# Scan block of a Mamba layer: exponentials of the decays written to SBUF, decay tiles multiplied in pairs

## The chip, the cores and the metric

One Trainium2 chip, one core of it. The time is the device time of one execution of the whole kernel in microseconds; the kernel before was run three times without the profiler, and one more execution was profiled.

## The reference

The kernel computes a decoder of four layers, each with three parts that are added to a residual x of 8 batches x 128 tokens x 128 features. The change touches only the first part, a Mamba block. Cut to what matters, with delta = softplus(...), u = silu(conv(...)) of 256 channels, and 64 states for each channel:

```python
A = -jnp.exp(A_log)
def step(h, inputs):
    d_t, B_t, C_t, u_t = inputs
    dA = jnp.exp(d_t[:, :, None] * A)
    h = h * dA + (d_t * u_t)[:, :, None] * B_t[:, None, :]
    y_t = jnp.einsum('bdn,bn->bd', h, C_t)
    return (h, y_t)
```

For each of 8 batches, 256 channels and 64 states there is a recurrence over 128 tokens: h is multiplied by the decay exp(delta * A), then delta * u * B is added; y sums h * C over the states.

## The kernel before, in words

`mamba_stage` (from L836) runs a norm, `mamba_inputs` (projections, convolution, softplus), `scan_block` (L1059), and `mamba_output` (gate, output projection, and early work of the next part). Engines run their own instruction streams and meet at semaphores.

`scan_block` works on 128 tiles: 8 batches (b) x 2 channel halves (c) x 8 tiles. A tile has 16 channels: its 128 partitions hold 2 channels (j) x 64 states, and its free axis 2 (s) x 4 (i) channels x 128 tokens, 1024 elements of 4 bytes. `place` (L1085) maps tile k to (b, c, side, q); side picks the lower or the upper 64 channels of a half. A unit is the 8 tiles of one (b, c). What each engine does for tile k:

- SP (L1088): waits until the scan of k-7 is done, then issues two DMAs that bring du = delta * u, each row spread over 64 partitions, from `du_rows` in HBM to one of the seven `ring` areas (XN, XNT, O, masked_cos, masked_sin, and two halves of pos_bias, all in SBUF and free at this time).
- POOL (L1106): multiplies the ring area by B in place (L1111) and counts `fed`.
- PE (L1114): `multiply(k)` makes A * delta, 8 products with a contraction over 32 rows each, into one of three PSUM areas `decay` (two banks each). It waits for `scanned` of k-3, since the scan reads the area. The 32 rows come from two of the four row strips, g = 2 side + s.
- ACT (L1171): takes the exponential in place in PSUM (L1200) and counts `decayed`.
- DVE (L1209): one `tensor_tensor_scan` (L1219) over the 1024 elements, state = decay * state + fed, from the PSUM area and the ring area to the buffer `h` of the unit (small_pack or h1, alternating). Token 0 of each channel has decay 0, set once by a memset of a column (L1211), which makes one instruction of the eight recurrences.

Once a unit is scanned, PE sums h * C over the states: `gather(n, part)` (L1131), 128 products of 32 columns, in four parts that stand behind the multiplications of four tiles. `Cz` holds C placed in zeros by ACT (`place_c`, L1172). ACT copies the sum (`copy_sum`), PE turns it back and adds D * u (`turn_back`, L1147), and ACT copies y over du (`copy_y`). The order on PE is the loop at L1162, on ACT the one at L1196; POOL, DVE and SP go tile by tile.

The prediction also speaks of three places outside the scan: the convolution (L974, DVE, with POOL preparing A_pairs and D_order in L1012 and L1014), du = delta * u (L1002, DVE), and the gate product of `mamba_output` (L1035, DVE) beside which POOL makes masked_cos and masked_sin (L794).

## Time and profile before

| | us |
|---|---|
| three runs, median (lowest to highest) | 1407.34 (1396.89 to 1410.18) |
| profiled execution, its own time | 1392.82 |
| span in the profile, first to last instruction | 1390.8 |
| PE busy, over the whole span | 1114.5 (80%) |
| DVE busy | 850.9 (61%) |
| POOL busy | 570.0 (41%) |
| ACT busy | 529.5 (38%) |

The mean granted clock of TensorE is 0.848 of 2.4 GHz. The page gives busy time and the costliest groups over the whole span; since the parts of the kernel have different limits, the scan block is read from windows, from the groups by line and from the timeline of its own stretch. In the timeline each line is one instruction or a merged run of them: its start, its length, the engine, the line of the code, what is written from what, and in brackets how long the engine had been idle and what it waited for. In the trace a fp32 product shows as two MATMUL records, so the 8 products of a tile are "x16".

### The profile page before, as it was taken

The numbers are of one execution on the slowest core, as the hardware profiler recorded it, in microseconds if no ns is written. First come the engines' busy times: TensorE is split into PE (matmuls) and PEld (weight loads), VectorE is DVE, ScalarE is ACT, GpSimd is POOL, SyncE is SP. The second block draws the span as 40 slices with busy tenths as digits, with TensorE's granted clock in tenths as the row PEclk, the third lists the DMA queues.
The fourth block names the chain that finished last, engine by engine and source line by source line (L and its number), as shares of the span: only waits on it lengthen the run. The fifth ranks groups of instructions, "written<-read, shape, count | busy, mean of one in ns | idle before, by whom it ended". The sixth has DMA issues, their size and how long they took to land. (4 is left out here: it accounts for less than half of the span.)

```text
span 1390.8 us, 29830 instructions
## 1 busy us (share of the span) xinstructions
PE 1114.5 (80%) x12054; PEld 800.1 (58%) x12065; DVE 850.9 (61%) x1500; ACT 529.5 (38%) x1322; POOL 570.0 (41%) x382
## 2 busy tenths in 40 slices
PE   5568898898887898999547598689476899866895
PEld 2158787887875454545336255545366454543695
DVE  6577888888884476366713476567512676755233
ACT  2433434434431363255114164156133565612121
POOL 4169988989864702210157310020434201000432
PEclk9656988888878599999869799699688998987998
DMA  2099687778855200000075100000365000000793
GB/s 105 0 207 216 196 214 206 203 208 211 204 168 198 65 1 1 0 1 2 1 201 182 33 2 1 1 1 1 116 199 185 1 2 1 1 1 23 259 302 99
DMA packets 74232, 139.75 MB, mean 100 GB/s; under 512 B 8129, under 2 KB 28369, under 8 KB 73745
## 3 DMA queue, kind: packets, MB, share of 16 engines
q1 hardware_dynamic: 70128, 129.67, 32.8%
q0 software_dynamic: 3968, 8.18, 1.6%
q8 instruction: 96, 1.57, 0.5%
q14 instruction: 40, 0.32, 0.1%
HBM read 128.06 MB, written 14.82 MB: 103 GB/s over the span
## 5 line engine op out<-in xcount | busy, mean ns | idle before, releaser
L658 ACT ACTIVATE shifted_a<-scores,nmax_a 128x128 f32<-128x128 f32 x768 | 208.5, 387 | 85.7 <-DVE nmax_a L624 85.7
L1125 PE MATMUL decay<-delta,A_pairs 32*128 32x127 f32 x2048 | 178.6, 335 | 49.2 <-DVE small_pack L1219 18.9
L1200 ACT ACTIVATE decay<-decay 128x1016 f32<-128x1016 f32 x128 | 128.7, 1010 | 197.8 <-PE decay L1125 197.8
L1125 PEld LDWEIGHTS decay<-delta,A_pairs 32*128 32x128 f32 x2048 | 155.5, 235 | 69.6 <-DVE small_pack L1219 23.6
L624 DVE TENSOR_REDUCE nmax_a<-scores 128x4 f32<-128x512 f32 x192 | 123.6, 686 | 108.3 <-PE scores L563 105.9
L361 POOL TENSOR_TENSOR rstd<-ve,neghalf 128x4 f32<-128x4 f32 x30 | 31.5, 1051 | 281.7 <-DVE ve L347 281.7
L630 DVE COPY PTs_a<-PT 128x512 f32<-128x512 f32 x192 | 123.6, 681 | 4.6 <-PE PT L571 4.6
L571 PE MATMUL PT<-mamba_pack,shifted_a 128*128 128x128 f32 x768 | 114.1, 293 | 4.3 <-DVE PTs_a L630 2.7
L1460 POOL DMA_INDIRECT results<-xs_s x76 | 73.0, 960 | 104.2 <-DVE xs_s L1632 96.6
L571 PEld LDWEIGHTS PT<-mamba_pack,shifted_a 128*128 128x128 f32 x768 | 88.5, 149 | 36.8 <-issue 20.1
L247 PE MATMUL norm_ps<-identb 128*128 128x512 bf16 x180 | 59.6, 446 | 52.2 <-DVE ve L347 51.5
L1111 POOL TENSOR_TENSOR pos_bias<-pos_bias,B 128x1024 f32<-128x1024 f32 x36 | 85.2, 2383 | 6.8 <-DMA pos_bias<-du_rows 6.7
L563 PE MATMUL scores<-KH_a,QT_a 32*128 32x512 f32 x256 | 76.4, 674 | 1.0 <-POOL KH_a L547 1.0
L580 PEld LDWEIGHTS PO<-PTs_a,V 128*32 128x32 f32 x1536 | 37.3, 111 | 64.3 <-issue 35.2
L547 POOL TENSOR_TENSOR KH_a<-KT_a,small_pack 128x512 f32<-128x512 f32 x24 | 24.9, 1041 | 119.6 <-PE scores L563 100.4
L1142 PE MATMUL Y<-small_pack,Cz 128*32 128x64 f32 x2048 | 63.2, 288 | 1.9 <-issue 1.9
L1142 PE MATMUL Y<-h,Cz 128*32 128x64 f32 x2048 | 62.8, 288 | 1.6 <-issue 1.0
L1111 POOL TENSOR_TENSOR XN<-XN,B 128x1024 f32<-128x1024 f32 x19 | 45.1, 2374 | 45.6 <-DMA XN<-du_rows 45.5
L580 PE MATMUL PO<-PTs_a,V 128*32 128x128 f32 x1536 | 62.4, 284 | 0.0
L247 PEld LDWEIGHTS norm_ps<-identb 128*128 128x128 bf16 x180 | 19.4, 113 | 74.2 <-DVE ve L347 54.7
L329 ACT ACTIVATE XNT<-norm_ps 128x512 f32<-128x512 f32 x12 | 7.2, 597 | 140.6 <-PE norm_ps L369 140.6
L1142 PEld LDWEIGHTS Y<-small_pack,Cz 128*32 128x32 f32 x2048 | 54.8, 134 | 7.2 <-issue 5.3
(395 smaller groups left out, 2238.3 us busy)
## 6 DMA issues: line engine op xcount, KB each, us to landing
pos_bias<-du_rows SPq DMA_DIRECT2D x72, 256.0 KB, 4.9
small_pack<-L3f_w SPq DMA_DIRECT2D x15, 768.0 KB, 5.0
XN<-du_rows SPq DMA_DIRECT2D x38, 256.0 KB, 5.1
XNT<-du_rows SPq DMA_DIRECT2D x38, 256.0 KB, 4.8
O<-du_rows SPq DMA_DIRECT2D x36, 256.0 KB, 4.9
masked_cos<-du_rows SPq DMA_DIRECT2D x36, 256.0 KB, 4.9
masked_sin<-du_rows SPq DMA_DIRECT2D x36, 256.0 KB, 4.8
small_pack<-L2f_w SPq DMA_DIRECT2D x15, 514.0 KB, 5.0
```

Of the source, the lines that this page charges most:

```text
L247: nc.tensor.matmul(out, m.identb[:], bcast_mid(m.identb[:], HG), start=True, stop=True)
L563: nc.tensor.matmul(scores[u % 4][:], QT[rows, b * S:(b + 1) * S], KH[b % 2][rows, :, :], start=False, stop=True).then_inc(m.scored, 1)
L571: t = nc.tensor.transpose(PT[u % 2][:, j, :], shifted[u % 4][:, j, :], ident)
L580: t = nc.tensor.matmul(PO[32 * j:32 * j + 32, g, :], m.V[:, b, g * HG + j, :], PTs[u % 4][:, j, :], start=True, stop=True)
L624: nc.vector.tensor_reduce(nmax[:, u % 4, :], scores[u % 4][:], AX.X, ALU.min).then_inc(m.maxed, 1)
L630: nc.vector.tensor_copy(PTs[u % 4][:], PT[u % 2][:]).then_inc(m.pt_copied, 1)
L658: t = nc.scalar.activation(shifted[u % 4][:, j, :], scores[u % 4][:, j, :], ACT.Exp, scale=-1.0, bias=nmax[:, u % 4, j:j + 1])
L1111: nc.gpsimd.tensor_tensor(x, x, bcast_mid(B2[:, b * S:(b + 1) * S], PER), ALU.mult).then_inc(fed, 1)
L1125: t = nc.tensor.matmul(decay[k % DEEP][:, s, i, 1:S], A_pairs[strip, c, 4 * q + i, :, :].rearrange("p j n -> p (j n)"), delta[strip, c, b ...
L1142: t = nc.tensor.matmul(Y[32 * i:32 * i + 32, n % 2, half, :], Cz[:, token, :], at_token[n % 2][:, :, token], start=(turn == 0), stop=(turn ...
L1200: nc.scalar.activation(x, x, ACT.Exp).then_inc(decayed, 1)
L1460: nc.gpsimd.indirect_dma_start(results, bass.IndirectOffsetOnAxis(ap=number, axis=0), xs[:, j, 0:D], None).then_inc(returned.sem, returned ...
```

## The change

The seven areas are split: the first two (XN and XNT) become `kept`, and the exponential writes from PSUM to `kept[k % 2]`; the ring for the fed values keeps five. The scan reads `kept` and the ring. PSUM areas are given back by ACT (`decayed`) instead of DVE (`scanned`), and ACT waits for the scan of k-2, whose `kept` area it takes. `place` is changed so that tiles 2p and 2p+1 are the two sides of one q, and `multiply(p)` makes both, 16 products that go around the four row strips, into two PSUM areas. The gather of a unit is cut into parts of 9, 9, 9 and 5 turns of four products (8 each before), one behind each pair; the copies on ACT move accordingly.

```diff
@@ -1063,7 +1063,8 @@
 
 
 
-    UNITS, PER, DEEP = B * IC, 8, 3
+    UNITS, PER, DEEP, KEPT = B * IC, 8, 3, 2
+    TURNS = [0, 9, 18, 27, 32]
     TILES = UNITS * PER
     with ExitStack() as ctx:
         sb = lambda name, shape, dt=F32: ctx.enter_context(nc.sbuf_tensor(name, shape, dt))
@@ -1072,8 +1073,9 @@
         flat = lambda a: a.rearrange("p b d -> p (b d)")
         ring = [flat(m.XN[:]), m.XNT[:], flat(m.O[:]), flat(m.masked_cos[:]), flat(m.masked_sin[:]),
                 flat(m.pos_bias[:, 0:H // 2, :]), flat(m.pos_bias[:, H // 2:, :])]
+        ring = [a.rearrange("p (s i t) -> p s i t", s=2, i=4) for a in ring]
+        ring, kept = ring[KEPT:], ring[:KEPT]
         R = len(ring)
-        ring = [a.rearrange("p (s i t) -> p s i t", s=2, i=4) for a in ring]
         Ys = [sb(f"Ys{k}", [128, 2, PAIRS]) for k in range(2)]
         decay = [ctx.enter_context(nc.psum_tensor(f"decay{k}", [128, 2, 4, S], F32)) for k in range(DEEP)]
         Y = ctx.enter_context(nc.psum_tensor("Y", [128, 4, 2, PAIRS], F32))
@@ -1082,7 +1084,7 @@
         multiplied, decayed, fed, scanned, c_placed, summed, sum_copied, sum_turned, y_copied, zeroed = (
             m.sem(f"scan_{n}") for n in ("multiplied", "decayed", "fed", "scanned", "c_placed", "summed",
                                          "sum_copied", "sum_turned", "y_copied", "zeroed"))
-        place = lambda k: (k // (2 * PER), k // PER % 2, k % PER // 4, k % 4)
+        place = lambda k: (k // (2 * PER), k // PER % 2, k % 2, k % PER // 2)
         block = ctx.enter_context(nc.Block())
 
         @block.sync
@@ -1112,21 +1114,20 @@
 
         @block.tensor
         def _(pe):
-            def multiply(k):
-                b, c, side, q = place(k)
-                if k >= DEEP:
-                    pe.wait_ge(scanned, k - DEEP + 1)
-                else:
-                    pe.wait_ge(zeroed, DEEP)
+            def multiply(p):
+                if 2 * p + 2 > DEEP:
+                    pe.wait_ge(decayed, 2 * p + 2 - DEEP)
+                b, c, _, q = place(2 * p)
                 for i in range(4):
-                    for s in range(2):
-                        g = 2 * side + s
+                    for g in range(4):
+                        side, s = g // 2, g % 2
                         strip = slice(32 * g, 32 * g + 32)
                         t = nc.tensor.matmul(
-                            decay[k % DEEP][:, s, i, 1:S],
+                            decay[(2 * p + side) % DEEP][:, s, i, 1:S],
                             A_pairs[strip, c, 4 * q + i, :, :].rearrange("p j n -> p (j n)"),
                             delta[strip, c, b * S + 1:(b + 1) * S], start=True, stop=True)
-                t.then_inc(multiplied, 1)
+                        if i == 3 and s == 1:
+                            t.then_inc(multiplied, 1)
 
             def gather(n, part):
                 b = n // IC
@@ -1135,12 +1136,12 @@
                     pe.wait_ge(c_placed, b + 1)
                     if n >= 2:
                         pe.wait_ge(sum_copied, n - 1)
-                half = part // 2
-                for turn in range(8 * (part % 2), 8 * (part % 2) + 8):
+                for turn in range(TURNS[part], TURNS[part + 1]):
+                    half = turn // 16
                     for i in range(4):
-                        token = 64 * half + 16 * i + turn
+                        token = 64 * half + 16 * i + turn % 16
                         t = nc.tensor.matmul(Y[32 * i:32 * i + 32, n % 2, half, :], Cz[:, token, :],
-                                             at_token[n % 2][:, :, token], start=(turn == 0), stop=(turn == 15))
+                                             at_token[n % 2][:, :, token], start=(turn % 16 == 0), stop=(turn % 16 == 15))
                 if part == 3:
                     t.then_inc(summed, 1)
 
@@ -1159,13 +1160,13 @@
                                              m.w("alternate")[:, rows], start=False, stop=True)
                 t.then_inc(sum_turned, 1)
 
-            for k in range(TILES + 18):
-                if k < TILES:
-                    multiply(k)
-                if k >= 11 and (k - 11) % 8 < 4 and (k - 11) // 8 < UNITS:
-                    gather((k - 11) // 8, (k - 11) % 8)
-                if k >= 17 and (k - 17) % 8 == 0 and (k - 17) // 8 < UNITS:
-                    turn_back((k - 17) // 8)
+            for p in range(TILES // 2 + 6):
+                if p < TILES // 2:
+                    multiply(p)
+                if p >= 9 and p % 4 == 1:
+                    turn_back((p - 9) // 4)
+                if p >= 5 and (p - 5) // 4 < UNITS:
+                    gather((p - 5) // 4, (p - 5) % 4)
 
         @block.scalar
         def _(act):
@@ -1193,30 +1194,35 @@
                 nc.scalar.activation(du[:, c, b * S:(b + 1) * S], YT[:, n % 2, :], ACT.Copy).then_inc(y_copied, 1)
 
             place_c(0)
-            for k in range(TILES + 19):
+            for k in range(TILES + 13):
                 if k < TILES:
                     act.wait_ge(multiplied, k + 1)
-                    x = decay[k % DEEP][:, :, :, 1:S].rearrange("p s i t -> p (s i) t")
-                    nc.scalar.activation(x, x, ACT.Exp).then_inc(decayed, 1)
-                if k % 16 == 8 and 0 < k // 16 < B:
+                    if k >= KEPT:
+                        act.wait_ge(scanned, k - KEPT + 1)
+                    else:
+                        act.wait_ge(zeroed, k + 1)
+                    nc.scalar.activation(kept[k % KEPT][:, :, :, 1:S].rearrange("p s i t -> p (s i) t"),
+                                         decay[k % DEEP][:, :, :, 1:S].rearrange("p s i t -> p (s i) t"),
+                                         ACT.Exp).then_inc(decayed, 1)
+                if k % 16 == 10 and 0 < k // 16 < B:
                     place_c(k // 16)
-                if k >= 15 and (k - 15) % 8 == 0 and (k - 15) // 8 < UNITS:
-                    copy_sum((k - 15) // 8)
-                if k >= 18 and (k - 18) % 8 == 0 and (k - 18) // 8 < UNITS:
-                    copy_y((k - 18) // 8)
+                if k >= 17 and k % 8 == 1 and (k - 17) // 8 < UNITS:
+                    copy_sum((k - 17) // 8)
+                if k >= 20 and k % 8 == 4 and (k - 20) // 8 < UNITS:
+                    copy_y((k - 20) // 8)
 
         @block.vector
         def _(dve):
-            for k in range(DEEP):
-                nc.vector.memset(decay[k][:, :, :, 0:1], 0.0).then_inc(zeroed, 1)
+            for k in range(KEPT):
+                nc.vector.memset(kept[k][:, :, :, 0:1], 0.0).then_inc(zeroed, 1)
             for k in range(TILES):
-                n = k // PER
-                out = h[n % 2][:, k % PER * T:(k % PER + 1) * T]
+                n, (_, _, side, q) = k // PER, place(k)
+                out = h[n % 2][:, (4 * side + q) * T:(4 * side + q + 1) * T]
                 dve.wait_ge(decayed, k + 1)
                 dve.wait_ge(fed, k + 1)
                 if n >= 2 and k % PER == 0:
                     dve.wait_ge(summed, n - 1)
-                nc.vector.tensor_tensor_scan(out, decay[k % DEEP][:].rearrange("p s i t -> p (s i t)"),
+                nc.vector.tensor_tensor_scan(out, kept[k % KEPT][:].rearrange("p s i t -> p (s i t)"),
                                              ring[k % R].rearrange("p s i t -> p (s i t)"), 0.0, ALU.mult,
                                              ALU.add).then_inc(scanned, 1)
 
```

On PE, at the start of the scan block, there stand before (each product shows one row, 128x127; `waits` names the semaphore):

```order
L1125 MATMUL decay<-delta,A_pairs 128x127 [waits scan_scanned]
L1125 MATMUL decay<-delta,A_pairs 128x127 x7
L1142 MATMUL Y<-small_pack,Cz 32x64 [waits scan_c_placed,scan_scanned]
L1142 MATMUL Y<-small_pack,Cz 32x64 x31
L1125 MATMUL decay<-delta,A_pairs 128x127 [waits scan_scanned]
L1125 MATMUL decay<-delta,A_pairs 128x127 x7
L1142 MATMUL Y<-small_pack,Cz 32x64 x32
```

and now:

```order
L1125 MATMUL decay<-delta,A_pairs 128x127 [waits scan_decayed]
L1125 MATMUL decay<-delta,A_pairs 128x127 x15
L1143 MATMUL Y<-small_pack,Cz 32x64 [waits scan_c_placed,scan_scanned]
L1143 MATMUL Y<-small_pack,Cz 32x64 x35
L1125 MATMUL decay<-delta,A_pairs 128x127 [waits scan_decayed]
L1125 MATMUL decay<-delta,A_pairs 128x127 x15
L1143 MATMUL Y<-small_pack,Cz 32x64 x36
```

Two tiles are multiplied in a row, the wait is on ACT's count, and a gather part has 36 products.

On DVE (the scan is listed as SCALAR_TENSOR_TENSOR) the first scans of the block were:

```order
L1211 MEMSET decay 128x8 x3
L1219 SCALAR_TENSOR_TENSOR small_pack<-decay,XN 128x1024 [waits scan_fed,scan_decayed]
L1219 SCALAR_TENSOR_TENSOR small_pack<-decay,XNT 128x1024 [waits scan_fed,scan_decayed]
L1219 SCALAR_TENSOR_TENSOR small_pack<-decay,O 128x1024 [waits scan_fed,scan_decayed]
L1219 SCALAR_TENSOR_TENSOR small_pack<-decay,masked_cos 128x1024 [waits scan_fed,scan_decayed]
```

and are now:

```order
L1217 MEMSET XN 128x8
L1217 MEMSET XNT 128x8
L1225 SCALAR_TENSOR_TENSOR small_pack<-XN,O 128x1024 [waits scan_fed,scan_decayed]
L1225 SCALAR_TENSOR_TENSOR small_pack<-XNT,masked_cos 128x1024 [waits scan_fed,scan_decayed]
L1225 SCALAR_TENSOR_TENSOR small_pack<-XN,masked_sin 128x1024 [waits scan_fed,scan_decayed]
L1225 SCALAR_TENSOR_TENSOR small_pack<-XNT,pos_bias 128x1024 [waits scan_fed,scan_decayed]
```

The number of scans and what they wait for are the same; their first input was PSUM (`decay`) and is SBUF (XN or XNT).

On ACT, in the middle of the block, the exponentials with the copies between them stood as follows:

```order
L1200 ACTIVATE decay<-decay 128x8x127 [waits scan_multiplied] x5
L1185 ACTIVATE Ys<-Y 128x128 [waits scan_summed]
L1200 ACTIVATE decay<-decay 128x8x127 [waits scan_multiplied] x3
L1193 ACTIVATE du<-YT 128x128 [waits scan_sum_turned]
```

and stand there now, with the placing of C (`Cz`) a tile further back:

```order
L1204 ACTIVATE XNT<-decay 128x8x127 [waits scan_scanned,scan_multiplied]
L1186 ACTIVATE Ys<-Y 128x128 [waits scan_summed]
L1204 ACTIVATE XN<-decay 128x8x127 [waits scan_scanned,scan_multiplied]
L1180 ACTIVATE Cz<-C 64x8x16 [waits scan_summed]
L1180 ACTIVATE Cz<-C 64x8x16
L1204 ACTIVATE XNT<-decay 128x8x127 [waits scan_scanned,scan_multiplied]
```

Each exponential had one wait, on PE's count, and has a second, on DVE's; it writes XN or XNT.

## Rows read from the trace of the kernel before

**Rows 1.** Windows of the kernel before: busy us of PE, PEld, DVE, ACT, POOL (xcount), PEclk, DMA share, GB/s
```profile
95.00:100.00 5.00, 4.53 (x36) 3.68 (x34) 4.96 (x3) 2.00 (x2) 5.00 (x3) 0.50 1.07 235
140.00:150.00 10.00, 9.11 (x220) 8.15 (x216) 7.92 (x5) 5.30 (x8) 8.09 (x4) 1.00 0.67 186
81.60:416.40 334.80, 297.79 (x6080) 266.67 (x6080) 285.79 (x128) 136.28 (x170) 300.27 (x128) 0.79 0.80 204
```

**Rows 2.** Timeline, first and last tile of the scan: start, length in us, engine, line
```profile
81.65 2.34 POOL L1111 TENSOR_TENSOR XN<-XN,B 128x1024 f32<-128x1024 f32 x1 [42.34 <-DMA XN<-du_rows]
...
414.12 2.29 DVE L1219 TENSOR_TENSOR_SCAN h<-decay,XNT 128x1024 f32<-128x1024 f32 x1 [0.69 <-ACT decay L1200]
```

**Rows 3.** Groups by line and shape, 0 to 420 us: busy us, mean ns, idle before, releaser
```profile
L1125 PE MATMUL decay<-delta,A_pairs 32*128 32x127 f32 x2048 | 178.6, 335 | 49.2 <-DVE small_pack L1219 18.9 <-DVE decay L1211 15.7 <-DVE h L1219 12.9
...
L1200 ACT ACTIVATE decay<-decay 128x1016 f32<-128x1016 f32 x128 | 128.7, 1010 | 197.8 <-PE decay L1125 197.8
...
L1111 POOL TENSOR_TENSOR XNT<-XNT,B 128x1024 f32<-128x1024 f32 x19 | 45.2, 2379 | 4.1 <-DMA XNT<-du_rows 4.0
...
L1219 DVE TENSOR_TENSOR_SCAN small_pack<-decay,XNT 128x1024 f32<-128x1024 f32 x9 | 20.5, 2275 | 2.7 <-ACT decay L1200 2.7
...
L1002 DVE TENSOR_TENSOR du<-delta,u 128x1024 f32<-128x1024 f32 x2 | 2.5, 1226 | 0.1
...
L932 ACT ACTIVATE u<-conv 128x1024 f32<-128x1024 f32 x2 | 2.1, 1048 | 8.5 <-DVE conv L974 8.5
```

**Rows 4.** Timeline, steady stretches of the scan block, all engines
```profile
93.31 1.23 SPq L1099 DMA_DIRECT2D masked_cos<-du_rows  x2
...
102.58 2.08 PE L1125 MATMUL decay<-delta,A_pairs 32*128 32x127 f32 x16 [0.22 <-DVE small_pack L1219]
...
106.88 1.99 PE L1142 MATMUL Y<-small_pack,Cz 128*32 128x64 f32 x64
...
107.55 2.38 POOL L1111 TENSOR_TENSOR masked_sin<-masked_sin,B 128x1024 f32<-128x1024 f32 x1
...
107.69 2.29 DVE L1219 TENSOR_TENSOR_SCAN h<-decay,masked_cos 128x1024 f32<-128x1024 f32 x1 [0.57 <-POOL masked_cos L1111]
...
411.88 1.16 PE L1125 MATMUL decay<-delta,A_pairs 32*128 32x127 f32 x16
```

**Rows 5.** Timeline, DVE and POOL behind the scan block, instruction by instruction
```profile
429.96 0.69 DVE L1035 TENSOR_TENSOR du<-du,gate 128x512 f32<-128x512 f32 x1 [13.54 <-PEq L1068]
430.56 0.68 DVE L1035 TENSOR_TENSOR du<-du,gate 128x512 f32<-128x512 f32 x1
431.07 2.03 POOL L794 TENSOR_TENSOR masked_cos<-O,small_pack 128x1024 f32<-128x1024 f32 x1 [0.50 <-ACT O L777]
431.17 2.49 DVE L1035 TENSOR_TENSOR du<-du,gate 128x512 f32<-128x512 f32 x1
433.07 2.44 POOL L794 TENSOR_TENSOR masked_sin<-O,small_pack 128x1024 f32<-128x1024 f32 x1
433.58 2.48 DVE L1035 TENSOR_TENSOR du<-du,gate 128x512 f32<-128x512 f32 x1
```

**Rows 6.** Timeline, DVE and POOL in the convolution
```profile
34.52 3.78 POOL L1012 TENSOR_TENSOR A_pairs<-A,mamba_pack 128x2048 f32<-128x2048 f32 x1
34.74 4.10 DVE L974 SCALAR_TENSOR_TENSOR conv<-padded,mamba_pack,conv 128x512 f32<-128x512 f32 x1
42.44 0.73 DVE L974 SCALAR_TENSOR_TENSOR conv<-padded,mamba_pack,conv 128x512 f32<-128x512 f32 x1
```

**Rows 7.** Groups by line, 75 to 430 us, and the page's DMA issues (KB, us to landing)
```profile
L1156 PE MATMUL YT<-u,D_order 128*64 128x64 f32 x128 | 15.0, 250 | 1.7 <-ACT Ys L1185 1.7
...
O<-du_rows SPq DMA_DIRECT2D x36, 256.0 KB, 4.9
```

**Rows 8.** Line L1219: what DVE waited for before its scans, us and times
```profile
  ACT decay L1200: 45.6, 47
  POOL XN L1111: 8.1, 1
```

## The prediction

> **What bounds the kernel now.** I read the page first: five engines, none busy over 80%, and the two costliest lines of the first third are in the scan block. The stage windows come next [rows 1]. The scan stage proper runs from the first POOL multiplication at 81.65 us to the end of the last scan, 414.12 + 2.29 = 416.4 us [rows 2]: 334.8 us for 128 tiles, 2.62 us a tile. In it POOL is busy 300.3 us, DVE 285.8 and PE 297.8. So three engines are near their limits and none is at it.
>
> The groups by line give what one tile costs [rows 3]: POOL multiplies by B in 2.38 us, DVE scans in 2.28 us, ACT takes the exponentials in 1.01 us, and PE makes the products. What DVE waits for is ACT, 45.6 us over 47 waits, against 8.1 us for POOL, all at the first tile [rows 8]; ACT waits 197.8 us for PE [rows 3]. The ring of waits is: the scan of tile k-3 frees a PSUM area, PE multiplies (2.08 us, or 1.16 us at the full clock [rows 4]), ACT exponentiates, DVE scans. When PE also gathers (1.99 us a part, in front of the next multiplication), the ring is late and DVE idles. The timeline shows the other thing that matters: the POOL multiplication and the scan run at the same time, POOL from 107.55 for 2.38 us and DVE from 107.69 for 2.29 us, both at their usual length [rows 4]. The stage lives from this overlap, since POOL and DVE together need 2.38 + 2.28 = 4.65 us a tile and get 2.62.
>
> **What the change removes.** PSUM areas are free after ACT (1.01 us) instead of after the scan (2.28 us), so PE runs ahead and the 45.6 us that DVE waits for ACT should go. Left alone, that makes POOL the bound: 128 x 2.377 = 304.3 us plus one last scan, 306.5 us, 28 us less than now.
>
> **What it adds: a scan with both inputs in SBUF.** So far the scan reads the decays from PSUM and the fed values from SBUF. Now it reads XN or XNT, and O or another ring area: two tensors in SBUF. No scan of this trace does that, so its cost is bounded from other instructions with two SBUF inputs that meet a POOL instruction reading SBUF. There are two places, and both say the same.
>
> At 430 us DVE multiplies du by gate, 512 elements, both in SBUF [rows 5]. The second of the four takes 0.68 us. The third starts at 431.17, just behind a POOL multiplication (431.07 for 2.03, so to 433.10), and takes 2.49 us: it ends at 433.66, 0.56 after POOL. The next POOL multiplication, same shape, starts at 433.07 while DVE is at work, and takes 2.44 us instead of 2.03: it ends at 435.51, 1.85 after DVE. The fourth DVE one starts at 433.58 and takes 2.48 us, to 436.06, 0.55 after POOL. So the two alternate and nothing overlaps but the ends: DVE saves 0.68 - 0.55 = 0.13 us of its own length and POOL 2.03 - 1.85 = 0.18. In the convolution the same [rows 6]: a DVE instruction of 0.73 us takes 4.10 us (34.74 to 38.84) behind a POOL one of 3.78 us (34.52 to 38.30), and ends 0.54 after it.
>
> The Trainium skill, page SBUF — State Buffer, section Who interferes with whom, states this as a rule: a VectorE instruction with two SBUF inputs fetches the second through the read interface that it shares with GpSimd, and against a GpSimd instruction that reads SBUF the later one is blocked fully until the first ends. The trace agrees (2.49 us for 0.68). Taken to the letter, without the saving at the ends, the rule gives the upper bound below.
>
> Applied to a tile: scan 2.276 - 0.13 = 2.14, POOL 2.377 - 0.18 = 2.19, together 4.33 us. They alternate, since the finished engine's next instruction queues behind the waiting one. The order of POOL and DVE changes in nothing but names and operands. Stage: first POOL multiplication alone 2.34, then 127 x 2.19 = 278.1, 127 scans x 2.14 = 271.8, last scan 2.28: 554.5 us. Against 334.8: **+219.7 us**. Ends of this term: above, no saving, 127 x 4.65 + 4.6 = 595.6, +261; below, both savings 0.2, as DVE's in the convolution (0.73 - 0.54), and POOL at its shortest (2.34 [rows 2]), 127 x (2.08 + 2.14) + 4.6 = 540, +205. I take the middle one because its rows have the same kind of POOL instruction and a full cycle.
>
> **The other edits, at 4.33 us a tile.** All cost nothing, and the slack is what hides them.
> - ACT writes SBUF instead of PSUM. The u row, 1024 elements SBUF to SBUF, is 1.05 us [rows 3]; 1.01 now. Bounds 0 to 0.05 us on an engine busy 1.0 of 4.33.
> - ACT now waits for the scan of k-2. Behind it stand the next exponential, the copies of Y and the placing of C; PE (for its PSUM area) and DVE wait for them. Exponential k can start when scan k-2 ends and is ready 1.05 later; scan k wants it 4.33 after that end. Slack 3.3 us, more than a copy's wait for one gather part (2.2 us).
> - PE works on pairs: 16 products over four row strips, then 36 gather products instead of 32. If four strips overlap no better than two, a pair costs 2 x 2.08 = 4.16 at 1.2 GHz, a part 1.99 x 36/32 = 2.24, turning back 1.9 us once in four pairs (twice the 15.0 us of one of its two lines, for 16 units [rows 7]): at most 8.3 us in the pair that has it and 6.4 in the others, of 8.66. If they do, less. It now waits for exponential 2p-2, which ends some 1.1 us after scan 2p-4; the product is needed by exponential 2p, when scan 2p-2 ends, 8.66 later. Cover goes only if the tile is under some 3 us. The clock here is 0.50 to 1.00 of 2.4 GHz [rows 1], and the sum above is with 1.2 GHz, so a colder PE is in it.
> - The ring has five areas for seven. A turn is scan end, 1.22 us issue [rows 4], 4.9 us to landing [rows 7], POOL and DVE 4.33, some 10.5 us; five tiles last 21.7. The DMA engines, at 1.07 of their time at 2.3 us a tile [rows 1], fall to about half.
> - Tile order within a channel pair, areas and the 9, 9, 9, 5 turns of the gather keep all counts. The tail behind the last scan has the same 128 gather products (some 8 us), so it stays at 13.5 us, to 429.96 [rows 5]. The load of small_pack goes out a few tiles ahead of the end as before.
>
> Sum: 1392.8 (profiled execution) + 219.7 = 1612.5 us. The three plain runs lie 4 to 17 us over the profiled one (median +14.5, 1407.3). Part of that may be waits in the stage that now have slack, so I add half: **1620 us**.
>
> **Rivals.**
> 1. *No blocking: the scan is exempt* and the change does what it removes. For it: the scan fetches slowly, 2.2 ns an element where a two-input multiplication needs 1.2 (1226 ns for 1024 [rows 3]), and no row shows a scan blocked. Against it: both places with two SBUF inputs show full exclusion. Time: stage 306.5 us if refills are all hidden; POOL waits 4.0 us for DMAs at XNT's 19 turns now [rows 3], so some 20 or more over the seven areas, and the ring is shorter, so 306 to 326; 315 gives 1373 in the profile's terms, 1387 as a median. This is the faster side; it decides if POOL keeps 2.38 us beside a scan. Chance 0.07.
> 2. *Shared by turns.* The scan leaves free the slots that it does not fetch in, so it costs POOL only 1.23 - 0.14 = 1.09 us: 2.19 + 1.09 = 3.28 a tile, stage 422, +87, 1480 us (1490 as a median). For it: the same slow fetch. Against it: in the rows one side stands still for all of the other's length. Chance 0.06.
> 3. *The bound moves to PE instead*, by its cold clock and the pair order: 8.3 us in the heaviest pair is under 8.66, so even then under 5 us in all. It is inside the range. That four strips do not run together is priced in there too; it changes nothing.
>
> On the first rival, the Trainium skill, page DVE: opcode table, instruction layouts, handler registers and perf-mode slots, section Datapath and trigger behaviour, says that the built-in tensor_tensor_scan carries a value back to an earlier stage and so runs at half throughput. The trace agrees (2276 ns for 1024 elements). The page doesn't say whether the read interface is held meanwhile; were it free half the time, the second rival's 1480 would follow.
>
> **How the numbers follow.** Forecast 0.86, first rival 0.07, second 0.06, else 0.01. Range of the forecast: 1598 (lower term) to 1654 (upper), with 0 to 17 us for the plain runs above; I give 1594 to 1660, which leaves out the rivals' 0.13. A measurement here tells about 1% from no change. Faster by over 1%: 0.06 (first rival but for its slow end), same 0.01, slower 0.93.
>
> **What would show it.** In the changed kernel's profile: scans or POOL multiplications of some 4.3 us at steady places, each ending 2.1 to 2.2 us behind the other's end, with both engines reported busy nearly throughout; the stage 555 us long; DMA share about 0.45; DVE's idle time for ACT gone; PE waiting for ACT. Scans of 2.28 beside POOL's 2.38 would prove me wrong, with the first rival; 3.3 us a tile, the second. If a tile takes over 4.7 us, some wait that I gave slack decides.

## The result, and the profile after

| | before | after |
|---|---|---|
| runs, median (lowest to highest), us | 1406.58 (1396.89 to 1410.18), 4 runs | 1624.16 (1619.73 to 1628.76), 4 runs |
| profiled execution, its own time | 1392.82 | 1619.73 |
| span | 1390.8 | 1618.0 |
| granted clock, mean of the span | 0.848 | 0.786 |

The kernel is slower by 15.6%: the ratio is 1.1558, with an interval of 1.1514 to 1.1601. The forecast was 1620 us, in a range of 1594 to 1660.

The timeline of the kernel after, some 220 us into the stage, answers to [rows 4]: start, length, engine, line, and in brackets the idle time before and its releaser.

```profile
299.23 4.33 POOL L1113 TENSOR_TENSOR masked_sin<-masked_sin,B 128x1024 f32<-128x1024 f32 x1
301.34 4.37 DVE L1225 TENSOR_TENSOR_SCAN small_pack<-XNT,masked_cos 128x1024 f32<-128x1024 f32 x1
...
301.51 1.02 ACT L1204 ACTIVATE XN<-decay 128x1016 f32<-128x1016 f32 x1 [3.29 <-DVE small_pack L1225]
...
302.58 2.09 PE L1125 MATMUL decay<-delta,A_pairs 32*128 32x127 f32 x32 [4.63 <-ACT XN L1204]
303.52 8.66 POOL L1113 TENSOR_TENSOR pos_bias<-pos_bias,B 128x1024 f32<-128x1024 f32 x2
...
305.63 4.40 DVE L1225 TENSOR_TENSOR_SCAN small_pack<-XN,masked_sin 128x1024 f32<-128x1024 f32 x1
```

POOL ends at 303.56, the scan at 305.71 (2.15 later), the next scan begins at 305.63. Both engines have nearly doubled lengths and no gap between instructions: a busy engine here is one that stands in line. That is the trap of this profile, because the shares of busy time say "DVE and POOL are fully used", while each works half of the time. The start of the stage shows which of the two is standing.

Timeline of the kernel after, first tiles and last scan:

```profile
79.41 2.34 POOL L1113 TENSOR_TENSOR O<-O,B 128x1024 f32<-128x1024 f32 x1 [42.48 <-DMA O<-du_rows]
81.84 2.29 DVE L1225 TENSOR_TENSOR_SCAN small_pack<-XN,O 128x1024 f32<-128x1024 f32 x1 [8.21 <-POOL O L1113]
81.90 4.38 POOL L1113 TENSOR_TENSOR masked_cos<-masked_cos,B 128x1024 f32<-128x1024 f32 x1 [0.16 <-DMA masked_cos<-du_rows]
...
86.24 2.35 POOL L1113 TENSOR_TENSOR masked_sin<-masked_sin,B 128x1024 f32<-128x1024 f32 x1
86.38 4.35 DVE L1225 TENSOR_TENSOR_SCAN small_pack<-XNT,masked_cos 128x1024 f32<-128x1024 f32 x1 [2.25 <-POOL masked_cos L1113]
...
627.95 2.26 DVE L1225 TENSOR_TENSOR_SCAN h<-XNT,masked_sin 128x1024 f32<-128x1024 f32 x1
```

The first scan begins 0.06 us before the second multiplication. It keeps its 2.29 us, and POOL takes 4.38 and ends 2.15 behind it. At 86.24 the order is the other way round: POOL, 0.14 us earlier, keeps 2.35, and the scan takes 4.35 and ends 2.14 behind POOL. So whoever starts first is undisturbed and the other gets all of the wait. From then on each instruction starts while the other engine is at work, and each pays: from the scan at 94.94 to the one at 619.38, 122 tiles later, it is 524.44 / 122 = 4.30 us a tile. The last scan, with no multiplication beside it, is back at 2.26.

The stage lasts from 79.41 to 627.95 + 2.26 = 630.2, which is 550.8 us against 334.8 [rows 2].

The scan line's waits in the kernel after (us, times), and who waited for it, answer to [rows 8]:

```profile
  POOL O L1113: 8.2, 1
  POOL masked_cos L1113: 2.2, 1
...
  ACT XN L1204: 207.2, 63
  ACT XNT L1204: 200.6, 63
```

The 45.6 us for ACT [rows 8] are gone, as intended, and ACT now waits for DVE. The same stretch in the groups by line (75 to 660 us: busy us, mean ns, idle before), and the window:

```profile
L1113 POOL TENSOR_TENSOR pos_bias<-pos_bias,B 128x1024 f32<-128x1024 f32 x50 | 215.9, 4338 | 0.0
L1125 PE MATMUL decay<-delta,A_pairs 32*128 32x127 f32 x2028 | 121.2, 406 | 224.9 <-ACT XN L1204 224.9
...
L1204 ACT ACTIVATE XN<-decay 128x1016 f32<-128x1016 f32 x64 | 65.1, 1017 | 207.2 <-DVE small_pack L1225 106.9 <-DVE h L1225 100.3
```

```profile
75.00:660.00 585.00, 283.48 (x6448) 247.97 (x6445) 561.09 (x165) 146.87 (x180) 558.76 (x142) 0.64 0.45 130
```

The exponential into SBUF takes 1.017 us (1.010 in place [rows 3]). PE waits 224.9 us and its granted clock over the stretch is 0.64 (0.63 over the stage alone, against 0.79 [rows 1]); in the trace nobody waits for its products. The DMA share is 0.45 (0.46 over the stage alone, against 0.80 [rows 1]), and the page has 4.3 us from issue to landing for O (4.9 [rows 7]).

The account of the spans, 1618.0 - 1390.8 = 227.2 us: the stage +216.0; its start 2.2 earlier; the tail between the last scan and the first gate product 9.4 us for 13.5, so -4.2; and the rest of the kernel behind that product 978.4 us for 960.8, +17.6. The last is probably not the change's: the code there is the same, and so is the granted clock, 0.87 in both traces. The kernels of the experiments below, the same in this part too, spend 950.2 to 982.1 us in it, by chip 970.6 to 982.1 (four traces), 955.7 to 966.0 (four), 950.2 to 963.7 (three) and 981.1 (one). Within one chip that is at most 13.4 us, less than the 17.6; but the whole kernel before varied by 17.4 us over its five executions (1392.82 to 1410.18), and the profiled one was the shortest of them. That chance made the 17.6 is argued from this, not shown. The medians, which smooth it, are 217.6 us apart.

### The profile page after: what moved, and what is told of

Read it like the earlier page. It is cut to its first block and busy times, and to the rows that moved or that the text cites. A ratio compares the mean times of both kernels' runs of the same rounds, so it can differ in the third digit from the quotient of the medians.

```text
span 1618.0 us, 29957 instructions
## 1 busy us (share of the span) xinstructions
PE 1076.1 (67%) x12054; PEld 761.1 (47%) x12065; DVE 1110.9 (69%) x1499; ACT 531.5 (33%) x1322; POOL 815.4 (50%) x382
## 5 line engine op out<-in xcount | busy, mean ns | idle before, releaser
L1125 PE MATMUL decay<-delta,A_pairs 32*128 32x127 f32 x2048 | 122.4, 406 | 240.4 <-ACT XN L1204 224.9
L1125 PEld LDWEIGHTS decay<-delta,A_pairs 32*128 32x128 f32 x2048 | 105.2, 297 | 256.9 <-ACT XN L1204 239.4
L1113 POOL TENSOR_TENSOR pos_bias<-pos_bias,B 128x1024 f32<-128x1024 f32 x50 | 215.9, 4338 | 0.0
L1204 ACT ACTIVATE XN<-decay 128x1016 f32<-128x1016 f32 x64 | 65.1, 1017 | 207.2 <-DVE small_pack L1225 106.9
L1113 POOL TENSOR_TENSOR O<-O,B 128x1024 f32<-128x1024 f32 x26 | 110.8, 4261 | 42.5 <-DMA O<-du_rows 42.5
L1204 ACT ACTIVATE XNT<-decay 128x1016 f32<-128x1016 f32 x64 | 65.2, 1019 | 200.6 <-DVE small_pack L1225 106.4
L1113 POOL TENSOR_TENSOR masked_cos<-masked_cos,B 128x1024 f32<-128x1024 f32 x26 | 112.9, 4340 | 0.2 <-DMA masked_cos<-du_rows 0.2
L1113 POOL TENSOR_TENSOR masked_sin<-masked_sin,B 128x1024 f32<-128x1024 f32 x26 | 110.8, 4261 | 0.0
```

The costliest lines, as they stand in the source:

```text
L1113: nc.gpsimd.tensor_tensor(x, x, bcast_mid(B2[:, b * S:(b + 1) * S], PER), ALU.mult).then_inc(fed, 1)
L1125: t = nc.tensor.matmul(decay[(2 * p + side) % DEEP][:, s, i, 1:S], A_pairs[strip, c, 4 * q + i, :, :].rearrange("p j n -> p (j n)"), delta ...
L1204: nc.scalar.activation(kept[k % KEPT][:, :, :, 1:S].rearrange("p s i t -> p (s i) t"), decay[k % DEEP][:, :, :, 1:S].rearrange("p s i t -> ...
```

## The experiments

Each was run beside the kernel before on the same chip, whose median differs by chip: 1405.5 us for SBUF alone, pairs alone, the product on DVE and POOL's writes; 1409.6 for the POOL instruction beside a scan from PSUM; 1391.4 to 1391.6 for all others. A ratio is given as it was estimated, with its interval; it can differ by up to 0.4% from the quotient of the two medians. The kernel before alone spreads by 18.6 to 24.1 us on one chip, so where there is one run only, the reading rests on the lengths of the instructions and not on the total. The theory: a scan with two SBUF inputs and a POOL instruction that reads SBUF exclude each other, one whole instruction after the other. Its rivals: the pair order on PE or the shorter ring costs the time; a scan from SBUF is slower by itself; any POOL access to SBUF does it; the two share by turns.

### SBUF areas alone, tile order of before

```diff
-                nc.vector.tensor_tensor_scan(out, decay[k % DEEP][:].rearrange("p s i t -> p (s i t)"),
+                nc.vector.tensor_tensor_scan(out, kept[k % KEPT][:].rearrange("p s i t -> p (s i t)"),
```

With it go the areas `kept`, the exponential's target and the waits of the change; products, gather and copies stay as before.

> Of the change only the two SBUF areas for the exponentials and the waits that go with them; tiles, products, gather and copies in the order of before. Exclusion theory (a scan with both inputs in SBUF and a POOL multiplication don't run at the same time): 4.30 us a tile, scans and multiplications of about 4.35 us, 1612 to 1630 us. Rival, the pair order and PE's new waits cost the time: scans of 2.28 us, about 1400 us.

Measured: 1617.5 us (2 runs), ratio 1.150 (1.143 to 1.157), beside 1.156 for the whole change. POOL and DVE alternate as there (start, length):

```profile
301.44 4.35 POOL L1112 TENSOR_TENSOR masked_sin<-masked_sin,B 128x1024 f32<-128x1024 f32 x1
...
303.57 4.37 DVE L1223 TENSOR_TENSOR_SCAN small_pack<-XNT,masked_cos 128x1024 f32<-128x1024 f32 x1
...
305.74 4.34 POOL L1112 TENSOR_TENSOR pos_bias<-pos_bias,B 128x1024 f32<-128x1024 f32 x1
```

The loss belongs to the areas in SBUF with the ring of five and the waits that go with them; the pair order has no part in it. Two kernels below, with the B product on DVE and with POOL only writing, keep all three and have scans of 2.27 to 2.29 us, so neither the place of the areas nor ring and waits alone make the loss.

### Pairs alone, exponentials in place in PSUM

```diff
-                if k >= DEEP:
-                    pe.wait_ge(scanned, k - DEEP + 1)
+                if 2 * p + 2 > DEEP:
+                    pe.wait_ge(scanned, 2 * p + 2 - DEEP)
```

Seven ring areas, the pair order, the gather parts and copies of the change.

> Of the change only the pairs from four row strips and the gather in four parts behind pairs; exponentials in place in PSUM, ring of seven, PE waits for the scans of 2p-2. Exclusion theory: scans 2.28 us and multiplications 2.38 us side by side; two of three PSUM areas must be free at once, so after scan 2p-2 come 2.09 us of products and 1.01 us of exponential against 2.28 us of the other scan: 2.5 to 2.75 us a tile, 1380 to 1425 us. Rival, the pair order costs the time: over 1550 us.

Measured: 1400.0 us (10 runs), ratio 0.997 (0.993 to 1.001): no difference. Timeline, one pair and the scan beside POOL:

```profile
199.43 2.38 POOL L1112 TENSOR_TENSOR XN<-XN,B 128x1024 f32<-128x1024 f32 x1
199.58 2.26 DVE L1221 TENSOR_TENSOR_SCAN h<-decay,masked_cos 128x1024 f32<-128x1024 f32 x1
...
204.30 1.17 PE L1126 MATMUL decay<-delta,A_pairs 32*128 32x127 f32 x32
```

POOL and the scan start 0.15 us apart and both keep their length. A whole pair, 16 products (x32), takes 1.17 us, as long as one tile of before (x16, 1.16 [rows 4]). The stage takes 326 us from first to last scan (84.5 to 410.65), 332 before. What DVE waits for now:

```profile
  ACT decay L1202: 30.8, 36
  POOL XN L1112: 8.5, 1
  PE Y L1144: 7.6, 14
```

PE lost 66 us of busy time in the window 75 to 430 (312.7 to 246.6), and DVE's wait for ACT only went from 45.6 to 30.8. PE now waits 90.6 us for scans in front of its products, where it waited 31.8 before: there are three areas for tiles made two at a time, a pair needs an area that the scan gives back late, and what PE saves in the products it spends waiting. A kernel with more areas was not run.

### The B product on DVE, POOL idle

```diff
-        @block.gpsimd
-        def _(pool):
-            for k in range(TILES):
...
+            feed(0)
             for k in range(TILES):
+                if k + 1 < TILES:
+                    feed(k + 1)
```

The changed kernel, its POOL instruction given to DVE in front of the scan.

> The changed kernel with the multiplication by B moved from POOL to DVE, one tile ahead of the scan; POOL has nothing to do in the block. Exclusion theory: the scan is 2.28 us again though both its inputs are in SBUF, the multiplication 1.23 us: 3.3 to 3.5 us a tile, about 1500 us, faster than the changed kernel although one engine does the work of two. Rival, a scan from SBUF is slow by itself (4.37 us): 5.5 us a tile, about 1770 us.

Measured: 1492.6 us (one run). Groups by line, one of the scan's forms:

```profile
L1226 DVE TENSOR_TENSOR_SCAN small_pack<-XNT,pos_bias 128x1024 f32<-128x1024 f32 x13 | 29.7, 2288 | 0.0
```

A scan of two SBUF inputs takes 2.29 us when POOL is idle, as one from PSUM does. It isn't slow by itself. The kernel also shows the price of the exclusion in another way: one engine doing both jobs in turn (3.31 us a tile) is 125 us faster than two engines that exclude each other (1617.5 us with the SBUF areas alone, on the same chip).

### POOL only writes

```diff
-                nc.gpsimd.tensor_tensor(x, x, bcast_mid(B2[:, b * S:(b + 1) * S], PER), ALU.mult).then_inc(fed, 1)
+                nc.gpsimd.memset(x, 0.01).then_inc(fed, 1)
```

This kernel leaves out the product with B: the ring is overwritten by a constant.

> The changed kernel with POOL's multiplication by B replaced by a memset of the same tile, so the product du * B is left out: a POOL instruction that writes SBUF and reads nothing. If only POOL's reads exclude the scan: scans of 2.28 us, 2.3 to 2.4 us a tile, 1355 to 1380 us. If any POOL instruction on SBUF does: 2.14 + 0.9 = 3.0 us a tile, about 1455 us. Rival, slow scan from SBUF: 4.3 us a tile, 1620 us.

Measured: 1374.5 us (one run). Timeline:

```profile
202.51 0.95 POOL L1113 MEMSET pos_bias<- 128x1024 f32 x1 [1.28 <-DMA pos_bias<-du_rows]
203.71 2.27 DVE L1225 TENSOR_TENSOR_SCAN small_pack<-XNT,pos_bias 128x1024 f32<-128x1024 f32 x1
...
204.68 0.96 POOL L1113 MEMSET pos_bias<- 128x1024 f32 x1 [1.21 <-DMA pos_bias<-du_rows]
```

The memset at 204.68 lies wholly inside the scan of 203.71 to 205.98, and neither is longer. POOL's writes alone don't collide; with its reads gone the collision is gone. This is what the Trainium skill, page SBUF — State Buffer, section Who interferes with whom, says of a GpSimd instruction that only writes. The run also gives a bound for what the change could be worth without exclusion: DVE's waits between scans fall to 15.5 us behind the first one, and the kernel takes 1374.5 us for 1405.5, but POOL's instruction is shorter here (0.95 us for 2.38). The ring of five areas and the new waits are in this kernel and in the one with POOL idle, so they don't cause the loss.

### POOL reads one operand

```diff
-                nc.gpsimd.memset(x, 0.01).then_inc(fed, 1)
+                nc.gpsimd.tensor_scalar(x, x, 0.01, None, ALU.mult).then_inc(fed, 1)
```

Here too the product with B is left out: a constant takes its place.

> The changed kernel with POOL's multiplication by B replaced by a multiplication with a constant: it reads and writes the same tile but no second tensor, so the product with B is left out. Exclusion theory, in which any POOL instruction that reads SBUF excludes the scan for its length: scans wait, the tile takes 2.14 us plus that instruction's own length (about 1 us for 1024 elements, by the casts of 2048 in 1.9 us), 3.0 to 3.4 us a tile, 1450 to 1510 us. Rival, two tensors on both sides are needed for a collision: scans of 2.28 us, below 1400 us.

Measured: 1430.6 us (one run), below the range that I gave. Timeline, the first tile and a steady place:

```profile
78.00 2.77 POOL L1113 TENSOR_SCALAR O<-O 128x1024 f32<-128x1024 f32 x1 [41.07 <-DMA O<-du_rows]
80.74 2.77 POOL L1113 TENSOR_SCALAR masked_cos<-masked_cos 128x1024 f32<-128x1024 f32 x1
80.87 3.05 DVE L1225 TENSOR_TENSOR_SCAN small_pack<-XN,O 128x1024 f32<-128x1024 f32 x1 [8.80 <-POOL O L1113]
...
199.57 3.00 POOL L1113 TENSOR_SCALAR masked_cos<-masked_cos 128x1024 f32<-128x1024 f32 x1
...
199.93 3.05 DVE L1225 TENSOR_TENSOR_SCAN h<-XN,O 128x1024 f32<-128x1024 f32 x1
...
202.54 3.01 POOL L1113 TENSOR_SCALAR masked_sin<-masked_sin 128x1024 f32<-128x1024 f32 x1
```

At first sight this is the pattern of the changed kernel with smaller numbers, and one could read the 2.98 us of a tile (the mean over the stage; here 199.57 to 202.54) as 2.14 for the scan and 0.84 for a short POOL instruction. The first row forbids it: with no scan beside it, the instruction takes 2.77 us. An exclusion would then need about 2.77 + 2.28 less some 0.3 at the ends, 4.75 us a tile. The scan that starts at 80.87, just behind a POOL instruction, ends 0.41 us behind it (83.92 against 83.51), where one that had stood still would end 2.14 behind. The two run side by side and disturb each other: 0.77 us for the scan, 0.24 for POOL.

The last run settled which of the readings holds.

### The same POOL instruction beside a scan from PSUM

```diff
-                nc.gpsimd.tensor_tensor(x, x, bcast_mid(B2[:, b * S:(b + 1) * S], PER), ALU.mult).then_inc(fed, 1)
+                nc.gpsimd.tensor_scalar(x, x, 0.01, None, ALU.mult).then_inc(fed, 1)
```

The edit is made to the kernel with pairs alone.

> The kernel with pairs alone (decays stay in PSUM, so the scan has one input in SBUF), with POOL's multiplication by B replaced by a multiplication by a constant, one operand read; the product with B is left out. In the earlier kernel with that POOL instruction and the decays in SBUF, the first POOL instruction, with no scan beside it, took 2.77 us, the later ones 3.01 and the scans 3.05, in a period of 2.98 us: much less than the 2.77 + 2.28 - 0.3 = 4.75 of a full exclusion. Theory A: one read operand does collide with the scan's second SBUF input, but only for part of its length (+0.24 us for POOL, +0.77 for the scan). Then here, without the second SBUF input, POOL keeps 2.77 us throughout and the scans 2.28, the tile takes 2.77 us by POOL, the stage 128 x 2.77 + 2.3 = 357 us, and the kernel some 1415 to 1430 us. Theory B: the longer times there have nothing to do with the two reads (the first instruction was short for another reason): POOL takes 3.0 us here too, the stage 386 us, the kernel 1445 to 1460 us. Theory C: such an instruction is about 0.85 us long and the other 2.14 us there were waiting: then POOL's instructions are near 0.85 us here and the stage falls to some 300 us, the kernel to 1370 to 1385.

Measured: 1431.2 us (one run), 1 us over the range of theory A; the instructions are those of theory A, the stage 352.7 us (82.31 to 435.05) for its 357. Timeline, start of the stage and a steady place:

```profile
85.05 2.77 POOL L1112 TENSOR_SCALAR XNT<-XNT 128x1024 f32<-128x1024 f32 x1
85.18 2.29 DVE L1221 TENSOR_TENSOR_SCAN small_pack<-decay,XN 128x1024 f32<-128x1024 f32 x1 [9.02 <-POOL XN L1112]
...
205.43 2.79 POOL L1112 TENSOR_SCALAR masked_cos<-masked_cos 128x1024 f32<-128x1024 f32 x1
205.59 2.29 DVE L1221 TENSOR_TENSOR_SCAN h<-decay,O 128x1024 f32<-128x1024 f32 x1 [0.45 <-POOL O L1112]
```

Without the second SBUF input POOL keeps 2.77 to 2.80 us and the scan 2.29, which waits for POOL (0.45). So theory C, the short instruction, and B fell. One read operand collides with the scan's second SBUF input, but for a part of the time only. The Trainium skill, page SBUF — State Buffer, section Summary: rules for kernel authors, has the second one to issue blocked fully until the first finishes; for the two-operand multiplication the rows agree (4.30 us a tile), for this instruction they don't (2.98, where full blocking would give about 4.75), and the measurement decides. Whether the number of operands or the kind of instruction makes the difference isn't told apart: both changed at once.

### Every second tile through SBUF

```diff
+                    to = kept[k // 2 % KEPT] if k % 2 == 0 else decay[k % DEEP]
...
+                of = kept[k // 2 % KEPT] if k % 2 == 0 else decay[k % DEEP]
```

The lines shown choose the area for the exponential and for the scan; the waits of PE, ACT and DVE are fitted to it.

> The pairs, with the exponentials of even tiles in SBUF and of odd tiles in place in PSUM. Exclusion theory: only the even scans and POOL's multiplications keep each other out, so a pair takes two multiplications of POOL (4.75 us) and one scan of 2.14 us, 6.7 to 6.9 us a pair, half of the way from before to the changed kernel: 1480 to 1515 us. If the stage merely followed PE's order or the ring of five, it would be at one of the ends.

Measured: 1469.8 us (one run), 78 over the kernel before, and 10 below the range that I gave. Timeline of one pair and a bit, DVE and POOL:

```profile
196.66 4.39 DVE L1231 TENSOR_TENSOR_SCAN small_pack<-XNT,pos_bias 128x1024 f32<-128x1024 f32 x1
198.86 4.32 POOL L1113 TENSOR_TENSOR masked_cos<-masked_cos,B 128x1024 f32<-128x1024 f32 x1
200.97 2.26 DVE L1231 TENSOR_TENSOR_SCAN small_pack<-decay,O 128x1024 f32<-128x1024 f32 x1
...
203.14 2.35 POOL L1113 TENSOR_TENSOR masked_sin<-masked_sin,B 128x1024 f32<-128x1024 f32 x1
...
203.28 4.35 DVE L1231 TENSOR_TENSOR_SCAN small_pack<-XN,masked_cos 128x1024 f32<-128x1024 f32 x1
```

In one kernel, beside the same POOL instruction, the scan from PSUM keeps 2.26 us beside POOL and the one from SBUF takes 4.39. The pair takes 6.62 us (196.66 to 203.28), the sum of one excluding round, 2.14 + 2.19, and one free scan, 2.28: 6.61. So the exclusion is priced by instruction, and it can be summed.

### The gather in six parts

What is a better change to the kernel before? Its DVE waits 45.6 us for ACT, when a gather part stands in front of the next products on PE. The first try made the parts smaller and spread them.

```diff
+    TURNS = [0, 6, 12, 17, 22, 27, 32]
...
-                if k >= 11 and (k - 11) % 8 < 4 and (k - 11) // 8 < UNITS:
-                    gather((k - 11) // 8, (k - 11) % 8)
+                if k >= 10 and (k - 10) % 8 < 6 and (k - 10) // 8 < UNITS:
+                    gather((k - 10) // 8, (k - 10) % 8)
```

> The kernel before with the gather of a unit in six parts of 6 or 5 turns behind tiles 10 to 15, instead of four parts of 8 behind tiles 11 to 14. Theory: in before DVE waits for ACT because a gather part of 1.99 us stands in front of the next tile's products; parts of 1.5 us take part of that away, but PE's work stays: 1395 to 1406 us. Rival, the loss is PE's total work at the low clock (about 3.3 us a tile at 1.2 GHz): no gain, 1400 to 1412 us.

Measured: 1455.8 us (4 runs), ratio 1.049 (1.042 to 1.057). The expectation was wrong, theory and rival. Windows, of this kernel and then of the kernel before (busy us of PE, PEld, DVE, ACT, POOL, granted clock, DMA share, GB/s):

```profile
150.00:400.00 250.00, 247.11 (x3927) 220.13 (x3928) 178.47 (x79) 85.46 (x107) 185.33 (x79) 0.50 0.59 166
```

```profile
150.00:400.00 250.00, 225.81 (x4860) 202.59 (x4864) 217.34 (x98) 106.69 (x136) 229.42 (x98) 0.84 0.80 207
```

With the work spread evenly PE is busy 99% of the time at a granted clock of 0.50, which is the 1.2 GHz level, for the whole stretch (and from 90 to 478 us as well). Before, with gaps between its blocks, the mean is 0.84. PE's work for a tile then takes 3.2 us (250 us for 79 scans), and PE is the bound. I had taken the clock for a given. Why the clock stays at the low level here isn't settled by these runs.

### Idle products to hold the clock

Would filling products raise the clock? If they did, they would pay. Two kernels, from the one with pairs alone (gather in 8, 8, 8, 8 turns), put idle bf16 products behind every second pair, four and eight of them. They write to a part of Y that nothing reads.

```diff
+                if p < TILES // 2 and p % 2 == 1:
+                    for _ in range(4):
+                        nc.tensor.matmul(Y[:, 2:4, :, :].rearrange("p a h x -> p a (h x)"), m.identb[:],
+                                         bcast_mid(m.identb[:], 2), start=True, stop=True)
```

> The pairs with exponentials in place in PSUM, and four idle products (128x128 by 256 columns, bf16, into an unused part of the Y area) behind every second pair. Theory: with the scan reading PSUM the stage lives from PE's clock, since a pair takes 2.09 us at 1.2 GHz and 1.17 us at 2.4 GHz between two scans; if the idle products hold the clock up, POOL's 2.38 us a tile is the bound: stage of 308 to 318 us, 1380 to 1392 us. Rival, the clock does not follow them or they only add PE work: 1398 to 1410 us.

> As with four idle products, but eight. If the clock follows activity: at least as high a clock as with four, 1378 to 1392 us, unless the idle products (0.9 us for eight at 2.4 GHz) delay the next pair. Rival: 1400 to 1415 us.

Measured: with four 1396.4 us (10 runs), ratio 1.0005 (0.996 to 1.005); with eight 1418.0 (4 runs), ratio 1.019 (1.012 to 1.025). The windows of the kernel with pairs alone, with four, and with eight:

```profile
150.00:400.00 250.00, 185.78 (x4920) 163.11 (x4916) 218.88 (x99) 104.79 (x136) 230.79 (x100) 0.86 0.77 206
```

```profile
150.00:400.00 250.00, 191.66 (x4897) 160.21 (x4898) 214.65 (x97) 103.19 (x133) 226.02 (x98) 0.84 0.76 204
```

```profile
150.00:400.00 250.00, 200.82 (x4617) 166.98 (x4619) 200.56 (x90) 95.66 (x123) 211.11 (x91) 0.82 0.71 190
```

PE's busy time goes up (185.8, 191.7, 200.8 us) and the granted clock doesn't (0.86, 0.84, 0.82). Two kernels without idle products, below, have 0.82 and 0.87 in this window, so the small steps mean nothing; what is shown is that there is no rise. By its ratio the kernel with four is the rival's, no gain, and the one with eight is 3 us above the rival's range: its products stand in front of the next pair. This theory fell. The pairs-alone kernel shown for comparison has parts of 9, 9, 9 and 5 turns and ran on another chip.

### Larger gather parts

```diff
-    TURNS = [0, 9, 18, 27, 32]
+    TURNS = [0, 10, 20, 30, 32]
```

Pairs alone, with 40 products in three of the parts of a unit and 8 in the last one.

> Pairs with exponentials in place in PSUM, gather parts of 10, 10, 10 and 2 turns for 9, 9, 9 and 5, so that a unit is summed earlier (14 scans waited 7.6 us for it). Theory: a few us off, ratio to before 0.990 to 0.998. Rival, longer parts delay the next pair at 1.2 GHz and take it back: 1.000.

Measured: 1382.7 us (10 runs), ratio 0.9967 (0.993 to 1.0005). Not told apart from the kernel before, nor from the parts of 9, 9, 9 and 5 (0.997). DVE waits 36.0 us for ACT in 40 places, and none for PE (7.6 with the smaller parts).

### Even tiles in halves

The exponentials of a pair come in the order even, odd, and DVE, done with the pair before, waits for the even one: two take 1.91 us, so it comes some 1 us behind PE's end. Here the even tile's exponential and scan are cut at the PSUM bank into two halves, so that the scan of the first half starts when half of the exponential is done. It is the kernel of the experiment before with one more edit.

```diff
-                    x = decay[k % DEEP][:, :, :, 1:S].rearrange("p s i t -> p (s i) t")
-                    nc.scalar.activation(x, x, ACT.Exp).then_inc(decayed, 1)
+                    for banks in (slice(0, 1), slice(1, 2)) if k % 2 == 0 else (slice(0, 2),):
+                        x = decay[k % DEEP][:, banks, :, 1:S].rearrange("p s i t -> p (s i) t")
+                        nc.scalar.activation(x, x, ACT.Exp).then_inc(decayed, 1)
```

> As with parts of 10, 10, 10, 2, and for even tiles the exponential and the scan in two halves of one PSUM bank each, so that the scan starts 0.4 us earlier behind a pair's products (DVE waited for ACT 30.8 us over 36 waits); DVE pays 0.14 us a pair. Theory: 5 to 15 us less than before, ratio 0.985 to 0.997. Rival, POOL at 2.38 us a tile and its DMAs bound it already: 1.000.

Measured: 1374.3 us (6 runs), ratio 0.986 (0.982 to 0.991). It beats both kernels, by 1.4% the one before. Timeline (the halves are merged, x2) and the scan line's waits:

```profile
202.65 1.98 ACT L1203 ACTIVATE decay<-decay 128x508 f32<-128x508 f32 x3 [2.43 <-PE decay L1126]
202.88 2.34 POOL L1112 TENSOR_TENSOR O<-O,B 128x1024 f32<-128x1024 f32 x1
203.49 2.31 DVE L1229 TENSOR_TENSOR_SCAN small_pack<-decay,pos_bias 128x512 f32<-128x512 f32 x2
```

```profile
  ACT decay L1203: 22.1, 35
  POOL XN L1112: 8.7, 1
  PE Y L1144: 3.8, 1
```

Two half scans take 2.31 us, only 0.03 more than one whole, and the exponentials of a pair 1.98 for 1.91. DVE's wait for ACT halves from 45.6 [rows 8] to 22.1 us. From the first scan to the end of the last the stage is 313.1 us (82.3 to 395.4), 332.3 before (84.1 to 416.4), and 324.9 without the halves (82.1 to 407.0): -19.2, of which the halves bring 11.8. The medians differ by 17.1, and by 8.4 from the kernel without the halves. The granted clock from 150 to 400 us was 0.87 with the halves and 0.82 without, so a part of the 11.8 may be the clock's; DVE's shorter wait for ACT, 22.1 for 36.0 us, with 3.8 for PE added, is 10.1 of them.

## Why the prediction was right

By its own steps:

- **Exclusion instead of overlap** was the step that carried the sum, and it holds. The sum had 4.33 us a tile, made of 2.14 and 2.19; the trace has 4.30, with the ends 2.14 us (the scan's) and 2.15 us (POOL's) apart at the two first meetings, so the small miss lies in POOL's term. The stage was to take 554.5 us and took 550.8; the difference is 0.03 x 128. The evidence was in the trace of before, in two places with other instructions [rows 5, 6]. The runs with POOL idle, with POOL only writing and with the scan from PSUM show that it takes both sides. They also draw a bound that I hadn't seen: it holds for POOL's multiplication of two operands, and not for its multiplication by a constant.
- **What the change removes** was right: DVE no longer waits for ACT. It is worth nothing in the changed kernel, since the exclusion covers it many times.
- **The edits costed at nothing** cost nothing. The exponential took 1.017 us (bound 1.05). The slack that I named for ACT, 3.3 us, shows as its wait in the timeline, 3.29 and 3.10. Ring and DMA: 0.45 of the engines' time as forecast, landing after 4.3 us, not 4.9; POOL waits for no refill after the second tile.
- **PE's pair** was bounded at 4.16 us; it took 2.09 at the low clock, as long as a single tile before. The four strips run together. It changed nothing here, since the bound already lay under the 8.66 us of a pair.
- **The tail** was to stay 13.5 us and took 9.4. In the trace of before, two gaps in it, of 1.05 and 2.03 us, are put down to issue, with a DMA share of 0.59 in the tail; after, the tail has no such gap and a share of 0.01: the load of small_pack went out 13.8 us before the end of the last scan (616.45), where it had been 4.4 (412.02). So the load moved against the tail, and I didn't price it. The traces of the experiments go with this: the tail is 9.4 us in the three kernels with a DMA share of at most 0.32 in it, 9.9 and 10.5 at 0.47 and 0.39, and 11.5 to 16.8 in the nine with 0.59 and more. That the load makes the gaps is still argued from these, as no run moved the load alone.
- **Half of 14.5 us** for the plain runs above the profiled one: the runs after have a median 4.4 us over the profiled, those before 13.8. Stage, tail and start make +209.6 us (216.0 - 4.2 - 2.2), and the medians are 217.6 apart; if the plain runs' stages are like the profiled ones, the 8 us between lie in the rest of the kernel; no trace of them shows it. Stage, tail and start came out 3.7, 4.2 and 2.2 us under the sum's 219.7, and the rest of the kernel made up for 8 of them. That the medians end up 2.1 us from the sum is in part luck. The range of 1594 to 1660 doesn't follow from its own terms either: 1598 and 1654 with 0 to 17 us on top are 1598 to 1671. The result lies in both.
- **Rivals.** No blocking would have been some 1387 us; the kernel in which POOL only writes comes near that case, at 1374.5, with a shorter POOL instruction. Sharing by turns asked for 3.28 us a tile, and the trace has 4.30. It was a better rival than its rows let it look: sharing of a kind is what the multiplication by a constant shows, 2.98 us a tile. The bound on PE didn't come: PE waits 224.9 us.

## What to carry to other kernels

Before an operand is moved from PSUM to SBUF, count the SBUF inputs of the VectorE instruction that reads it: with one, the scan of this case ran beside GpSimd (2.26 us beside 2.38); with two, it and a two-operand GpSimd multiplication from SBUF take turns, whole instruction by whole instruction, and both look busy. The price can be summed from the undisturbed lengths (here 2.14 + 2.19 us a tile forecast and 4.30 measured, for 2.62), and the neighbours in the old trace that have two SBUF inputs already show it. What a chain of engines waits for may be better shortened by cutting the first piece of work: halves of every second tile, left in PSUM, brought 1.4% together with the pairs and the larger gather parts; the halves without the pairs were not run.

## What the runs showed that I had not expected

- Sixteen products with a contraction over 32 rows, going round four row strips and into four PSUM banks, took 2.09 us at a granted clock of 0.50 and 1.17 at 1.00; eight over two strips took 2.08 and 1.16 [rows 4].
- The collision has degrees. A POOL instruction that only writes runs inside a scan without any cost (0.96 us, scan 2.27); one that multiplies by a constant costs the scan 0.77 us and itself 0.24; one that multiplies two operands stands still, or makes the scan stand still, until the other has ended, and then needs all but 0.14 us (the scan) or 0.23 us (POOL) of its own length.
- With a steadier stream of products, PE busy 99%, the granted clock stood at 0.50 for all of a window of 250 us, where the same products in blocks with gaps had a mean of 0.84; and idle bf16 products didn't raise it. What decides it stays open.
- The rest of the kernel, the same code each time, took from 950.2 to 982.1 us in the profiled executions, and up to 13.4 us apart on one chip. A single profiled span is no measure for differences of a per cent; the stage inside it, read by itself, leaves this part out.
